# A tanh scan with four PSUM banks, and two banks for every other matrix product

## The reference, cut to what matters

```python
p = patches(x)                                   # (32, 196, 768)
h = layernorm(layernorm(p, g1, b1) @ W + bias, g2, b2)
h = concatenate([h, txt], axis=1)                # (32, 273, 256)
x_sub = rmsnorm(_layernorm(h)[:, ::2]) * g_norm  # every second token
x_proj, gate = split(x_sub @ w_in.T + b_in, 2)
def step(s, xt):                                 # 137 steps, one after another
    s = tanh(s * A + xt[:, :, None] * Bm)        # state (32, 256, 64)
    return s, s @ Cm.sum(axis=0) + Dv * xt
y = scan(step, zeros, x_proj)
a = (y * silu(gate)) @ w_out.T + b_out
h = h + repeat(a, 2, axis=1)[:, :273]
n = _layernorm(h)
h = h + (silu(n @ wg.T) * (n @ wu.T)) @ wd.T     # hidden width 768
```

## Time and profile before

| what | value |
|---|---|
| median of three runs | 1422.66 us |
| the profiled execution, its own time | 1424.49 us |
| its span | 1422.6 us |
| mean granted TensorE clock | 0.963 |
| TensorE busy | 1248.4 us (88%) |
| VectorE busy | 1079.0 us (76%) |
| ScalarE busy | 1010.4 us (71%) |
| GpSimd busy | 439.5 us (31%) |

### The profile page before, as it was taken

One profiled execution on the slowest core, in us unless ns is written; L12 is line 12 of the kernel. 1 busy time (PEld: TensorE's weight loads), 2 busy tenths in 40 slices (PEclk: granted clock), 3 DMA queues, 4 the chain that ended last, 5 costly groups with the idle time before them and its releaser, 6 DMA issues.

```text
span 1422.6 us, 25915 instructions
## 1 busy us (share of the span) xinstructions
PE 1248.4 (88%) x7199; PEld 642.3 (45%) x7199; DVE 1079.0 (76%) x2401; ACT 1010.4 (71%) x1955; POOL 439.5 (31%) x443
## 2 busy tenths in 40 slices
PE   3858899999999999999999999999889989988865
PEld 1623345454545454545444445454344444433333
DVE  4638788888878787878787878787888888878621
ACT  1446786868686868787878786877877778768612
POOL 5303152515161615242424343423212122121121
PEclk8769999999999999999999999999999999999987
DMA  7230414141414142332324141303232232231210
GB/s 184 65 66 19 112 29 115 32 112 33 109 33 109 45 97 62 80 78 64 88 54 104 38 111 31 98 7 108 56 89 72 55 105 56 65 81 53 53 52 7
DMA packets 154926, 100.52 MB, mean 71 GB/s; under 512 B 129088, under 2 KB 143296, under 8 KB 153536
## 3 DMA queue, kind: packets, MB, share of 16 engines
q1 hardware_dynamic: 154880, 99.95, 28.1%
HBM read 58.85 MB, written 41.06 MB: 70 GB/s over the span
## 4 chain that ended last, share of the span: by engine, by line
PE 36%; issue 22%; ACT 12%; DVE 9%; DMA 8%; POOL 6%; SPq 3%; ACTq 0%; DVEq 0%; POOLq 0%
PE U L1114 7%; PE Y L1124 7%; DVE U L693 5%; ACT h L881 4%; PE P L1259 4%; DMA y_scr<-y_fx 4%; PE P L1260 4%; PE P L1199 3%; PE P L1168 3%; PE P L1274 2%; PE P L1275 2%; DMA yT<-y_scr 2%; POOL raw_s L1006 2%; DVE act L810 2%; SPq L582 1%
## 5 line engine op out<-in xcount | busy, mean ns | idle before, releaser
L693 DVE TENSOR_TENSOR U<-h,a_col 128x512 f32<-128x512 f32 x1096 | 722.6, 690 | 182.4 <-ACT h L881 175.9
L881 ACT ACTIVATE h<-U 128x512 f32<-128x512 f32 x1096 | 626.9, 598 | 221.3 <-PE U L1114 216.8
L1114 PE MATMUL U<-x_diag,b_st 128*128 128x512 f16 x1096 | 389.8, 387 | 80.7 <-DVE U L693 68.3
L1124 PE MATMUL Y<-h,read_st 128*32 128x512 f32 x2192 | 296.5, 613 | 0.3 <-ACT h L881 0.3
L1114 PEld LDWEIGHTS U<-x_diag,b_st 128*128 128x128 f16 x1096 | 104.9, 99 | 336.3 <-DVE U L693 275.8
L1056 POOL TENSOR_TENSOR xT_act<-act,xT_act 128x448 f16<-128x448 f32 x120 | 127.7, 1071 | 196.8 <-ACT xT_act L965 196.7
L1168 PE MATMUL P<-tok_w,xT_act 128*112 128x256 f32 x672 | 171.1, 387 | 1.6 <-ACT xT_act L898 1.6
L1168 PEld LDWEIGHTS P<-tok_w,xT_act 128*112 128x112 f32 x672 | 117.8, 179 | 53.5 <-issue 21.8
L1274 PE MATMUL P<-down_w,xT_act 128*112 128x256 bf16 x480 | 114.9, 277 | 4.9 <-POOL xT_act L1056 4.9
L1275 PE MATMUL P<-down_w,xT_act 128*112 128x256 bf16 x480 | 113.7, 275 | 0.0
L810 DVE SCALAR_TENSOR_TENSOR act<-fsg,P 128x448 f32<-128x448 f32 x120 | 73.9, 615 | 41.0 <-PE P L1260 28.4
(11 more groups left out here) (136 smaller groups left out, 1485.7 us busy)
## 6 DMA issues: line engine op xcount, KB each, us to landing
raw<-in_x SPq DMA_DIRECT2D x42, 448.0 KB, 6.2
tok_scr<-tok SPq DMA_DIRECT2D x20, 448.0 KB, 3.3
gate_scr<-gate_o SPq DMA_DIRECT2D x20, 448.0 KB, 2.5
gate_fx<-gate_scr SPq DMA_DIRECT2D x20, 448.0 KB, 5.3
res<-tok_scr SPq DMA_DIRECT2D x20, 448.0 KB, 3.6
out<-res SPq DMA_DIRECT2D x76, 112.0 KB, 2.3
x_diag<-scan_scr SPq DMA_DIRECT2D x320, 16.0 KB
x_diag<-scan_scr SPq DMA_DIRECT2D x304, 12.0 KB
```

What stands on the lines that cost most here:

```text
L693: dve.tensor_tensor(U[bank_of(slot)][:, :].rearrange("p (l b) -> p l b", b=B), h[:, c, :].rearrange("p (l b) -> p l b", b=B), a_col[:, c * ...
L881: sc.activation(h[:, c, :], U[bank_of(slot)][:, :], ACT.Tanh, scale=1.0 / U_SCALE).then_inc(squashed, 1)
L1114: pe.matmul(U[bank_of(slot)][:, :], b_st[:, c, :], x_diag[:, c, :, t * B:t * B + B], start=False, stop=True, skip_group_check=True).then_i ...
L1124: mm = pe.matmul(Y[c4 * 32:c4 * 32 + 32, :], read_st[:, t, half, :], h[:, half * RG + c4, :], start=(j == 0), stop=(t == steps - 1), skip_ ...
```

## The change

1. `NU` is 4: the scan has four banks. With 56 slots in a body the numbering runs on over the edge of a body, and every grow waits for the squash four slots back.
2. All other products use two banks, `P[0]` and `P[1]`. The parts of `turn` alternate between them, so part n waits for the copy of part n-2 (before: n-3). The new waits write down one fixed order of users of each bank. Readouts stay four products at a time.
3. b_out is one bf16 product of 96 rows by 512 columns for both halves: ones against a table with the bias as three bf16 pieces in rows 0, 32 and 64. VectorE makes the table in the setup, with eleven more instructions.
4. The gate has its own buffer `gate_in`. Its load waits for `z_done` of the group before, and is issued ahead of `y_scr` and not behind it.
5. The plans and the order on GpSimd are new in all kinds of body. `gate_silu` in image bodies moves from slot 55 to 47, the second half of `project` from 47, 55 to 47, 47, `attend` from slot 16 to 14, `residual` from 20 to 18, `shrink` from slots 0 to 6 to slots 2 to 4; in body 20 `residual` moves from slot 23 to 36, behind its 32 scanning slots.

The diff, cut to its core (of the plans only two lines of the image body are shown):

```diff
-NU = 3
+NU = 4
+BIASP = 96
+XA_AFTER, X_AFTER, GATE_AFTER = 1, 2, 4
...
-        shrink=(0, 0, 0, 1, 2, 4, 4, 6), turn=(7, 9, 9, 10, 13, 13, 14, 14), attend=(16, 16), average=(23, 27),
+        shrink=(2, 2, 3, 3, 3, 3, 4, 4), turn=(4, 8, 8, 9, 11, 11, 13, 14), attend=(14, 14), average=(19, 22),
...
-        P = [ctx.enter_context(nc.psum_tensor(f"P{n}", [128, 512], FP32)) for n in range(3)]
+        P = [ctx.enter_context(nc.psum_tensor(f"P{n}", [128, 512], FP32)) for n in range(2)]
...
+            own(dve.memset(bias_one[:, :], 1.0))
+            own(dve.memset(bias_row[:, :], 0.0))
+            dve.wait_ge(s_own, count[0])
+            own(dve.tensor_copy(bias_row[0:1, :], rows[0:1, 3, :]))
+            for p0 in (32, 64):
+                own(dve.tensor_copy(bias_row[p0:p0 + 1, :], rows[p0:p0 + 1, 3, :]))
+                dve.wait_ge(s_own, count[0])
+                own(dve.tensor_tensor(rows[p0:p0 + 1, 3, :], rows[p0:p0 + 1, 3, :], bias_row[p0:p0 + 1, :], ALU.subtract))
...
             if post:
+                sp.wait_ge(gate_wr, (q + 1) * 16)
+                sp.sem_inc(passed, 1)
+                if due(q):
+                    sp.wait_ge(z_done, q)
+                    sp.sem_inc(passed, 1)
+                sp.dma_start(gate_in[:, :].rearrange("p (a n) -> p a n", a=2), gate_scr[q]).then_inc(gate_ld, 16)
                 sp.wait_ge(y_out, q + 1)
...
-                if due(q * HB):
-                    sp.wait_ge(ffn_u_ps, q * HB)
-                    sp.sem_inc(passed, 1)
-                sp.dma_start(gate_fx[:, :].rearrange("p (a n) -> p a n", a=2), gate_scr[q]).then_inc(gate_ld, 16)
...
         def turn_bank(n):
-            return (2, 1, 0)[n % 3]
+            return n % 2
...
-                if n >= 3:
-                    pe.wait_ge(xT_done, g * 8 + n - 2)
+                if n >= 2:
+                    pe.wait_ge(xT_done, g * 8 + n - 1)
...
+                if k == 0:
+                    pe.matmul(P[0][0:PT, 0:2 * D], bias_one[:, :], bias_row[:, :].unsqueeze(1).to_broadcast([BIASP, 2, D]),
+                              start=True, stop=False, skip_group_check=True)
                 for j in range(DB):
                     mm = pe.matmul(P[0][0:PT, k * D:k * D + D], zT[:, j, k * PT:k * PT + PT], out_w[:, j, :],
-                                   start=(j == 0), stop=False)
-                mm = pe.matmul(P[0][0:PT, k * D:k * D + D], cst[0:PT, C_ID:C_ID + PT], rows[:, 3, :], start=False, stop=True)
+                                   start=False, stop=(j == DB - 1), skip_group_check=True)
```

188 lines of the change are left out of this document (105 added, 83 removed).

## The result

The changed kernel takes 1433.47 us (median of five runs, 1430.16 to 1436.58), beside 1422.49 for the kernel before. The ratio is 1.0083, with a 95% interval of 1.0066 to 1.0100: slower by 0.8%. The forecast was 1384, faster by 2.7%, with a range of 1350 to 1412. The prediction was wrong, in sign and in size.

The account below looks back on a forecast made before the run. TensorE was taken as nearest to the bound, its busy time holding exposed latency. Text bodies -21, image bodies -18, setup +1.5 and the end -1 gave -38.5 from 1424.49, so 1386.0, as median 1384 us; range 1350 to 1412.

Parts of the forecast that it names:

- The fourth bank in text bodies: Text bodies: grows waiting four slots back save 2.9 us a body, half of TensorE's 5.9 of waits with restarts.
- The bias: TensorE's stream: four fp32 records become one bf16 record, 0.64 us less in each of 20 groups.
- Setup and the end: Setup: VectorE's added instructions cost +1.5 us; from body 20 on the time changes by -1.
- The arrival at `attend`: Image bodies: TensorE reaches `attend` 18.0 us into the body, no gain, bounds 16.5 and 20.5.
- Rival 3: Image bodies: two banks of `turn` make ScalarE and TensorE hold each other, +2.3 us a body, 1441 as median; chance 0.12.
- The way of y: Image bodies: the gate's load ahead of `y_scr` makes `zT` 1.3 us later, at 20.0, bounds 17.4 and 21.
- `attend` ends at 20.0 + 0.17 + 1.95 = 22.1: Image bodies: after `zT` at 20.0 the attention product takes 1.95 us and ends 22.1 us into the body.
- rival 5: All 18 bodies: the new rhythm of waits lowers the granted clock, +14 us in all, 1398; chance 0.03.
- 2.4 lost instead of 4.9: Image bodies behind the attention product: the residual's wait and half of the old waits lose 2.4 us, before 4.9.
- The residual's wait: Image bodies: grow 19, queued behind `residual` and its late rows, makes TensorE wait 0.6 us.
- The sum for an image body: Image bodies 2 to 13: 67.1 us against 68.6, -1.5 a body, bounds 65.0 and 69.6.

Follow-up runs that it names:

- experiment 6: Changed kernel with the bias as two fp32 products again, without the table of the setup: 1436.69 us, ratio 1.0102 to the kernel before.
- experiment 1: Changed kernel with the gate's load issued behind `y_scr` again, own buffer kept: 1418.03 us, ratio 0.9979 to the kernel before.
- experiment 9: Kernel before with only the gate's own buffer and its load ahead of `y_scr`, behind the raw patches: 1439.53 us, ratio 1.0138.
- experiment 13: Changed kernel with the gate's load first in the body, ahead of the wait for the normalisation and the raw load: 1419.02 us, ratio 0.9981.
- experiment 8: Changed kernel with the raw patches loaded behind `yT` and their statistics in slots 15 to 20: 1443.60 us, ratio 1.0144.
- Experiment 3: Changed kernel with ten unused bf16 products of 512 columns on TensorE before the wait for `zT` in image bodies: 1425.34 us, ratio 1.0023.
- experiment 10: Changed kernel with gate load behind `y_scr`, ten idle products (loop only), last four `embed` parts and second `tok_stats` earlier: 1411.83 us, ratio 0.9922.
- 18: As 16, with `turn_fx` and its copy at slot 33 instead of 31: 1408.30 us, ratio 0.9913 to the kernel before.
- 17: Changed kernel with `residual` at slot 20 instead of 18 and nothing else: 1432.47 us, ratio 1.0090 to the kernel before.
- 15: As experiment 13, with `residual` at slot 20 instead of 18: 1409.34 us, ratio 0.9914 to the kernel before.
- 16: As 15, with ten idle products before the wait for `zT`, in loop bodies only: 1406.84 us, ratio 0.9899 to the kernel before.
- experiment 4: Changed kernel, four banks, but from body 3 on grows wait for the squash three slots back: 1535.74 us, ratio 1.0809 to the kernel before.
- experiment 2: Changed kernel with `attend` back at slot 16 instead of 14 in image bodies: 1427.76 us, ratio 1.0060 to the kernel before.
- experiment 11: Changed kernel with SyncE's queue ordered `y_scr`, raw patches, gate, `yT`: 1439.69 us, ratio 1.0130 to the kernel before.

## Why the prediction was wrong, point by point

- **The fourth bank in text bodies: right in direction, in size partly by luck.** Forecast -2.9 without the bias, measured -2.9 in all. I had taken half of 5.9 with no reason for just that half, and the measured number holds the bank and the new plan together. TensorE's waits for grows fell by 2.8 us. VectorE's wait for banks, which I wanted under 4, is 4.4 us.
- **The bias: too large.** 0.64 a body forecast. It is 0.9 in image bodies at half clock, and 0.1 in text bodies, where other work covers it (experiment 6).
- **Setup and the end: not to be told from one execution each.** VectorE's write of the readout table moved from 31.02 to 33.82 and the memset behind it from 33.77 to 34.96: +1.2 of +1.5. Body 20 on: -1.3 for -1. The first drive itself came at 84.0, 3.7 us later, but the start of body 2 is the same to 0.1. By the scatter named above neither number confirms the forecast.
- **The arrival at `attend`: right.** +17.9 for +18.0; TensorE waited 0.4 us for copies of `turn` in the whole body. Rival 3 named the nearest time, 1441, and by the wrong mechanism: that it came near is luck.
- **The way of y: the mechanism right, the size off by half.** `zT` at +20.7 for +20.0: 2.0 us later than before instead of 1.3. Moving the load costs 1.4 (experiments 1 and 9). In the changed kernel half of that is SyncE issuing `y_scr` later, at +6.1 (+5.3 in experiment 1); in experiment 9 it goes out at +5.6 as before, and all of it lies between `y_scr` and `yT`. Most of the other 0.6 fits the raw load itself, issued at +3.45 instead of +3.0, where I had it 0.5 us earlier; no run moved it alone. The Trainium skill, "DMA: Bandwidth & Descriptors", section "Queues, rings and completion order", says that each DMA engine takes descriptors in ring order. The orders tried agree with it, and not with mixed packets, by which the place of the gate would not have mattered: what is issued right ahead of a leg of y delays that leg, by 1.4 us for the 448 KB of the gate (experiment 1 against the changed kernel) and by some 5 us for all raw patches (`zT` at +19.2 in experiment 13, at +14.5 in experiment 8). The gate issued 5.0 us earlier still (experiment 13) did no harm.
- **The first step that failed: "`attend` ends at 20.0 + 0.17 + 1.95 = 22.1".** I priced the wait as its own length and the product behind it at full speed. It stands at half clock: 3.49 us for eight records instead of 1.89 in the body shown, and a low stretch at this place in every loop body. The product ended at +24.4 there and at +23.8 in the mean. Experiment 3 took that away and gained 0.6% with `zT` unchanged. I had rival 5 for the clock, but as a thing of all bodies by 0.8 us, with a chance of 0.03, and tied to the banks; it belongs to the wait that I myself forecast at 2 us.
- **The second step that failed: "2.4 lost instead of 4.9" behind the product.** The loss did not change: 47.3 us against 47.1. I halved it because VectorE's waits for banks would halve. They did, 8.6 to 4.6 us over the body, but TensorE gained nothing by it: behind the product it waited 1.6 us for grows before, and waits 0.8 for grows and 1.0 for the bank of `turn_fx` now. Taking that bank wait away brought longer waits for grows (1.1 us less and 0.6 more in experiment 10, 0.4 less and 0.4 more in 18), and bodies no more than 0.2 us shorter. What makes grows late there is then VectorE's own work; which part of it was not taken apart. In body 13, without patch statistics, the stretch behind the product takes 45.9 us, near the forecast 45.0, and took 46.9 in the kernel before. That fits, but y comes 6 us earlier in this body too, so it is no proof that the patch statistics are the cause.
- **The residual's wait, "0.6":** hidden in the changed kernel (17), and 1.1 us a body as soon as the product is in time (15 against 13).
- **The sum for an image body:** 67.1 forecast, 71.7 measured in the body shown. Of the 4.6 us, 0.7 is `zT`, 1.6 the product at half clock and 2.3 the stretch behind it. It is above my upper bound of 69.6; the clock had no term in the sum.

Why the time is what it is, then: text bodies, body 13 and the end brought 20.1 us; the loop lost 27.0, body 2 another 2.0. Of the loop's 2.7 us a body, 1.7 come back by the order of two transfers alone (experiment 1), and with the clock and the residual repaired as well (16) the body stands at 68.7, 0.2 under the kernel before. So even then this plan with its four banks gives next to nothing in image bodies. Left open is what a plan could do about VectorE's statistics: the two places I tried (8 and 10) moved the wait and did not remove it, and 8 did so with raw patches that came late. That the fourth bank is what helps the text bodies, and not their new plan, is argued from the waits and not shown: experiment 4 can't separate the two.

## What to carry to other kernels

Price a new wait of TensorE by what runs behind it too: a wait of 2 to 3 us in front of a product can halve the clock for the product, and filling it with idle matmuls cost 0.2 us a body at most here (16 against 15; where there was no wait, in body 13, they cost 2.3 us). When a buffer of its own frees a load, that load should leave the busy stretch of the queue and not merely change places in it; follow every leg of a round trip through memory, since bytes moved from ahead of one leg may stand ahead of the next. And a wait of one engine that went down counts only as far as the bounding engine waited for it: work out what becomes of TensorE's waits, not of VectorE's. Where an edit is meant to move a transfer, read in its trace that the transfer moved.

## What the runs showed of the hardware that I had not expected

- The clock: TensorE idle for 2.9 to 3.3 us at one place of a body of 71.6, with little idle else, was followed by 3.4 us at 1.2 GHz in nine bodies of nine; 1.6 to 2.0 us by the same in four, three and one of nine (experiments 1, 13, 15). With 0.6 to 0.9 us behind ten idle products it fell in none of nine (experiment 3), but with 0.9 to 1.1 us and no such products in six (experiment 2). In experiment 11 it fell in nine of nine with no idle time at `zT`, behind a wait of 3.7 us for a grow some slots before. So the length of the last wait alone does not decide. In the changed kernel each low stretch of a loop body lasted 3.4 us. One that was over before TensorE's operand was there cost 0.3 us at most (bodies 5, 7 and 9 of experiment 9).
- A 448 KB load that was issued 5.0 us ahead of 1.3 MB (experiment 13) left `zT` exactly where it was with the load behind `y_scr` (experiment 1), at +19.2: ahead of everything and behind everything cost the same, only between cost 1.4 us more.
